# Adding up the kinds of edges in another stage of a graph and mixture-of-experts kernel

## The reference, cut to what matters

```python
edge_index = jnp.stack([src, dst])
xn = _layernorm(x, axis=-1)
x = x + _L0_gnn_ref(xn, edge_index, edge_type_8, ...) + _L0_mix_ref(xn[None], ...)[0]
x = x + _L0_ffn_ref(_layernorm(x, axis=-1)[None], ...)[0]
```

```python
self_idx = jnp.arange(num_nodes, dtype=edge_index.dtype)
ei = jnp.concatenate([edge_index, jnp.stack([self_idx, self_idx], axis=0)], axis=1)
row, col = (ei[0], ei[1])
deg = jnp.zeros((num_nodes,), dtype=h.dtype).at[row].add(1.0)
deg_inv_sqrt = deg ** (-0.5)
norm = deg_inv_sqrt[row] * deg_inv_sqrt[col]
```

## Time and profile before

| | before |
|---|---|
| median of 3 runs | 2826.07 us (2821.76 to 2828.15) |
| the profiled execution, its own time | 2828.88 us |
| its span | 2827.1 us |
| PE busy | 2438.5 us, 86% |
| PE weight loads (beside the products) | 1990.5 us, 70% |
| DVE busy | 1542.4 us, 55% |
| ACT busy | 910.1 us, 32% |
| GpSimd busy | 673.1 us, 24% |
| mean granted clock of PE | 0.93 of full |
| HBM traffic over the span | 148 GB/s |

### The profile page before, as it was taken

The page is one execution under the profiler, slowest core; times in us unless marked ns, Lnnn a source line. Parts: engine busy times, 40 slices in busy tenths (PEclk is TensorE's granted clock), DMA queues, the critical chain, the costliest instruction groups (busy, mean ns, idle before and its releaser), DMA issues.

```text
span 2827.1 us, 32184 instructions
## 1 busy us (share of the span) xinstructions
PE 2438.5 (86%) x12218; PEld 1990.5 (70%) x12218; DVE 1542.4 (55%) x2412; ACT 910.1 (32%) x1115; POOL 673.1 (24%) x408
## 2 busy tenths in 40 slices
PE   5898897889999999987888789886949999987775
PEld 4777796667777777766677678775737789775654
DVE  4897334323332333246799787655953234567674
ACT  2222232111111111121366666514723212225341
POOL 3355401200000000011244343204521100226451
PEclk9999999989999999999899899987979999998888
DMA  4144441522221221134787978557833322436561
GB/s 119 45 107 117 118 143 64 162 64 78 82 78 57 83 82 38 53 114 165 236 286 262 285 257 287 196 173 235 288 135 129 103 68 67 149 115 239 191 224 62
DMA packets 170651, 406.79 MB, mean 144 GB/s; under 512 B 70935, under 2 KB 71249, under 8 KB 170468
## 3 DMA queue, kind: packets, MB, share of 16 engines
q1 hardware_dynamic: 94598, 336.90, 35.6%
q0 software_dynamic: 20144, 41.82, 4.6%
q10 hardware_dynamic: 55726, 25.60, 3.4%
HBM read 360.49 MB, written 56.80 MB: 148 GB/s over the span
## 4 chain that ended last, share of the span: by engine, by line
PE 57%; DVE 19%; DMA 12%; issue 4%; ACT 3%; ACTq 2%; SPq 1%; DVEq 1%; POOL 1%; POOLq 0%
PE PS L290 12%; PE PS L291 12%; PE PS L292 11%; PE PS L1173 7%; DVE low L282 6%; PE PS L951 4%; DMA q_rows<-leaf_rows_k 2%; ACT high L269 2%; PE PS L546 1%; DVE expert_stats L332 1%; ACTq L479 1%; PE PS L1424 1%; PE PS L2226 1%; DMA x_base<-in_x 1%; PE PS L1789 1%
## 5 line engine op out<-in xcount | busy, mean ns | idle before, releaser
L269 ACT ACTIVATE high<-raw 128x1024 fp32r<-128x1024 f32 x532 | 542.7, 1055 | 431.2 <-PE PS L292 290.1
L282 DVE TENSOR_TENSOR low<-raw,high 128x1024 fp32r<-128x1024 f32 x388 | 574.5, 1506 | 165.2 <-ACT high L269 162.4
L290 PE MATMUL PS<-high,xt_high 128*125 128x512 f32 x1280 | 520.0, 406 | 57.7 <-DVE low L282 14.8
L291 PE MATMUL PS<-low,xt_high 128*125 128x512 f32 x1280 | 513.3, 401 | 0.0
L292 PE MATMUL PS<-high,xt_low 128*125 128x512 f32 x1280 | 511.4, 400 | 0.0
L282 POOL TENSOR_TENSOR low<-raw,high 128x1024 fp32r<-128x1024 f32 x144 | 373.4, 2593 | 488.7 <-ACT high L269 477.6
L290 PEld LDWEIGHTS PS<-high,xt_high 128*125 128x125 f32 x1280 | 242.5, 189 | 123.6 <-issue 19.8
L292 PEld LDWEIGHTS PS<-high,xt_low 128*125 128x125 f32 x1280 | 241.9, 189 | 62.9
L291 PEld LDWEIGHTS PS<-low,xt_high 128*125 128x125 f32 x1280 | 242.3, 189 | 57.9
L1206 DVE TENSOR_TENSOR y_low<-PS,y_high 125x512 fp32r<-125x512 f32 x80 | 55.3, 692 | 296.5 <-ACT y_high L1195 296.5
L1195 ACT ACTIVATE y_high<-PS 125x512 fp32r<-125x512 f32 x80 | 47.8, 598 | 525.0 <-PE PS L292 525.0
(11 more groups left out here) (508 smaller groups left out, 4298.9 us busy)
## 6 DMA issues: line engine op xcount, KB each, us to landing
raw<-in_L_ffn_ew SPq DMA_DIRECT2D x96, 512.0 KB, 5.8
raw<-in_L_gnn_weight SPq DMA_DIRECT2D x64, 512.0 KB, 5.8
raw<-in_L_ffn_k_w SPq DMA_DIRECT2D x64, 512.0 KB, 7.1
raw<-in_L_ffn_q_w SPq DMA_DIRECT2D x64, 512.0 KB, 10.9
raw<-in_L_ffn_v_w SPq DMA_DIRECT2D x64, 512.0 KB, 9.1
raw<-in_L_ffn_f_w SPq DMA_DIRECT2D x64, 512.0 KB, 7.3
adjacency<-a_stage ACTq DMA_DIRECT2D x10, 1250.0 KB
a_kind<-adjacency POOLq DMA_DIRECT2D x8, 1525.9 KB, 18.5
```

The costliest lines, as they stand in the source:

```text
L269: a.e.activation(HIGH[i % NHIGH][:, 0:w], RAW[PLACE_OF[i]][:, 0:w], ACT.Copy).then_inc(*a.step(part_high, 1, [("high", i)]))
L282: v.e.tensor_tensor(LOW[p][:, 0:w], RAW[p][:, 0:w], HIGH[i % NHIGH][:, 0:w], ALU.subtract).then_inc(*v.step(signal, 1, [("low", i)]))
L290: p.e.matmul(dst, xh[:, kt, xs], wh[:, c], start=first and j == 0, stop=False)
L291: p.e.matmul(dst, xh[:, kt, xs], wl[:, c], start=False, stop=False)
```

## The change

The sum over the kinds, its degrees and its transpose leave the counting stage. GpSimd adds nothing there and makes only the low parts 0 to 5 in the start; parts 6 to 27 become DVE's, which makes them at the end of each bucket's turn. DVE adds one kind at a time to a tile of 125 x 3125 in the relations, behind `y_low` of tile 10r + 9, from the `a_kind` tile that the aggregate reads. The degrees, and five blocks of 125 for the transpose, stand in the gates and are stored between the loads of SP. The tile of the sum takes room of four places, so the rings of places change from part 33 on, and with them the moments at which SP may load.

```diff
     RINGS = [(0, EARLY + [12, 13]),
-             (33, [7, 8, 9, 10, 11, 6, 12, 13, 0, 1, 2, 3, 4, 5]),
-             (107, [6, 0, 1, 2, 3, 4, 5, 7, 8, 9, 10]),
-             (131, LEAF_K + LEAF_Q + LAST + [1, 2, 3, 4, 5, 7, 8, 9, 10, 6, 0]),
-             (200, LEAF_Q + LAST + [1, 2, 3, 4, 5, 7, 8, 9, 10, 6, 0]),
-             (250, [1, 2, 3, 4, 5, 7, 8, 9, 10, 6, 0]),
-             (329, AFTER_K + LAST + [3, 4] + ROUTED + [5] + BASE),
-             (369, LAST + [3, 4, 5] + BASE)]
+             (33, [6, 0, 1, 2] + LAST + [3, 4, 5]),
+             (107, [3, 4, 5, 6, 0, 1, 2]),
+             (127, [7, 8, 9, 10]),
+             (131, LEAF_K + LEAF_Q + LAST + [2, 3, 4, 5, 6, 0, 1, 7, 8, 9, 10]),
+             (200, LEAF_Q + LAST + [2, 3, 4, 5, 6, 0, 1, 7, 8, 9, 10]),
+             (250, [2, 3, 4, 5, 6, 0, 1, 7, 8, 9, 10]),
+             (329, AFTER_K + LAST + [4, 5] + ROUTED + [6] + BASE),
+             (369, LAST + [4, 5, 6] + BASE)]
...
     def low_on_gpsimd(i):
-        return i < 28 or i in (123, 124, 125) or 126 < i < 388 and i % 4 == 3 or i > 438 and i % 2 == 1
+        return i < 6 or i in (123, 124, 125) or 126 < i < 388 and i % 4 == 3 or i > 438 and i % 2 == 1
...
-    def turn_sum_tensor(p, c):
-        ps = bank(6, 2).rearrange("p (m c) -> p m c", c=128)[0:64, 0:TT, 0:PT]
-        p.wait_ge(at("kinds", c), at("target", c - 1) if c else at("bounds"))
-        for m in range(TT):
-            ins = p.e.transpose(ps[:, m, :], ALLC[c % 3][:, m, :], ident[0:PT, 0:PT])
-        ins.then_inc(*p.mark("sum turned", c))
...
-            if b % 4 == 2 and b >= 10:
-                turn_sum_tensor(p, b // 4 - 2)
...
             if j == 0:
-                a.wait_ge(*[at("adj stored", c - 2), at("kinds", c - 2)] if c > 1 else [at("many"), at("bounds")])
+                a.wait_ge(*[at("adj stored", c - 2)] if c > 1 else [at("many"), at("bounds")])
...
+        low_parts(v, fill_to(1, 1))
...
+            low_parts(v, fill_to(3 + h, 1))
+        low_parts(v, fill_to(5, 1))
...
-    def turn_sum_vector(v, c):
-        e, ps = v.e, bank(6, 2).rearrange("p (m c) -> p m c", c=128)[0:64, 0:TT, 0:PT]
-        v.wait_ge(at("kinds", c), at("degree", c - 1) if c else at("degree one"))
-        e.tensor_reduce(deg[:, 1, :], ALLC[c % 3][:, :, :], axis=AX.X, op=ALU.add).then_inc(*v.mark("summed", c))
-        v.wait_ge(v.last)
-        e.tensor_tensor(deg[:, 0, :], deg[:, 0, :], deg[:, 1, :], ALU.add).then_inc(*v.mark("degree", c))
-        v.wait_ge(at("sum turned", c))
-        if c > 1:
-            v.wait_ge(at("adjt stored", c - 2))
-        e.scalar_tensor_tensor(TA[c % 2][:, :, :], iota16[0:64, 0:N].rearrange("p (m c) -> p m c", m=TT), tgt[:, c:c + 1], ps,
-                               op0=ALU.is_equal, op1=ALU.add).then_inc(*v.mark("target", c))
...
-            if b % 4 == 2 and b >= 10:
-                turn_sum_vector(v, b // 4 - 2)
             if b % 2 == 0 and b:
                 fill_out_vector(v, 5 + b // 2)
-        for n in range(25, 30):
-            fill_out_vector(v, n)
-        turn_sum_vector(v, 8)
-        turn_sum_vector(v, 9)
-        v.wait_ge(v.last)
-        rsqrt(v, deg[:, 0, :], dis[:, :], lnt[:, 6, :], lnt[:, 7, :], "degree root")
+            low_parts(v, fill_to(6 + b // 2, b % 2))
+        for n in range(26, 30):
+            low_parts(v, fill_to(n, 0))
+            fill_out_vector(v, n - 1)
+            low_parts(v, fill_to(n, 1))
+        fill_out_vector(v, 29)
...
-        g.wait_ge(g.last)
-        e.iota(tgti[:, :], [[64, 10]], base=0, channel_multiplier=1).then_inc(*g.mark("target iota"))
...
-        low_parts(g, fill_to(0, 1))
-        fill_out_gpsimd(g, 0)
-        low_parts(g, fill_to(1, 1))
-        fill_out_gpsimd(g, 1)
-        for h in range(2):
-            fill_out_gpsimd(g, 2 + h)
-            low_parts(g, fill_to(3 + h, 1))
-        low_parts(g, fill_to(5, 1))
+        low_parts(g, 6)
...
     def edges_gpsimd(g):
         e = g.e
-        fill_out_gpsimd(g, 4)
-        fill_out_gpsimd(g, 5)
-        for b in range(NB):
-            if b % 4 == 3:
-                c = b // 4
-                stg, total = STG[c % 2], ALLC[c % 3][:, :, :]
-                g.wait_ge(at("copied", b), at("many"), at("bounds"))
-                if c > 2:
-                    g.wait_ge(at("sum turned", c - 3), at("summed", c - 3))
-                g.wait_ge(g.last)
-                e.tensor_tensor(total, stg[:, :, 0, :], stg[:, :, 1, :], ALU.add).then_inc(*g.mark())
-                for r in range(2, 8):
-                    g.wait_ge(g.last)
-                    e.tensor_tensor(total, total, stg[:, :, r, :], ALU.add).then_inc(*g.mark(*("kinds", c) if r == 7 else ()))
-            if b % 2 == 0 and b:
-                fill_out_gpsimd(g, 5 + b // 2)
-            low_parts(g, fill_to(6 + b // 2, b % 2))
-        for n in range(26, 30):
-            low_parts(g, fill_to(n, 1))
+        for n in range(4, 10):
+            fill_out_gpsimd(g, n)
...
-    def turn_sum_sync(s, c):
-        s.wait_ge(at("target", c), s.before(tas[c % 2]))
-        s.e.dma_start(adjt[64 * c:64 * c + 64, :], TA[c % 2][:, :, :].rearrange("p m c -> p (m c)")).then_inc(*s.lands(tas[c % 2], "adjt stored", c))
...
             n = 6 + b // 2
-            if b % 4 == 2 and b >= 10:
-                turn_sum_sync(s, b // 4 - 2)
             if n % TT == TT - 1:
                 load_parts(s, 9 + 4 * (n // TT) + (2, 4)[b % 2])
         load_parts(s, 33)
-        turn_sum_sync(s, 8)
-        turn_sum_sync(s, 9)
...
     def counted():
 
-        return [at("adj stored", 8), at("adj stored", 9), at("counts stored", 18), at("counts stored", 19), at("adjt stored", 8),
-                at("adjt stored", 9), at("degree root"), at("root stored", 28), at("root stored", 29), at("k", 9)]
+        return [at("adj stored", 8), at("adj stored", 9), at("counts stored", 18), at("counts stored", 19), at("own column"), at("root stored", 28), at("root stored", 29), at("k", 9)]
...
     def mix0_sync(s):
         load_parts(s, 38, *counted())
-        load_parts(s, 46)
...
-                    load_parts(s, 50 + 4 * h)
+                    load_parts(s, 46 + 4 * h)
...
     GROUPS = [(r, h) for r in range(8) for h in range(2)]
+
+
+    ASUM = place("a_sum", [PT, TT, N], F32, SPARE)
+    TA = place("at_stage", [PT, TT, PT], F32, SPARE + 12512)
+    tgt = const("target_id", [PT, TT], F32)
...
+    def add_kind(v, r):
+        a = AR[r % 2][:, :, 0:N].bitcast(F32)
+        v.wait_ge(at("kind", r), v.last)
+        if r:
+            v.e.tensor_tensor(ASUM[:, :, :], ASUM[:, :, :], a, ALU.add).then_inc(*v.mark("kinds", r))
+        else:
+            v.e.tensor_copy(ASUM[:, :, :], a).then_inc(*v.mark("kinds", r))
+
+    def degrees_vector(v):
+        v.wait_ge(at("target iota"))
+        v.e.tensor_copy(tgt[:, :], tgti[:, :]).then_inc(*v.mark())
+        v.e.tensor_reduce(deg[:, :], ASUM[:, :, :], axis=AX.X, op=ALU.add).then_inc(*v.mark())
+        v.wait_ge(v.last)
+        v.e.tensor_scalar(deg[:, :], deg[:, :], 1.0, None, op0=ALU.add).then_inc(*v.mark())
+        v.wait_ge(v.last)
+        rsqrt(v, deg[:, :], dis[:, :], lnt[:, 6, :], lnt[:, 7, :], "degree root")
+
+    def turn_sum_tensor(p, j):
+        ps = bank(6, 2).rearrange("p (m c) -> p m c", c=128)[0:PT, 0:TT, 0:PT]
+        p.wait_ge(at("kinds", 7), at("target", j - 1) if j else at("xl", "u", 4))
+        for m in range(TT):
+            ins = p.e.transpose(ps[:, m, :], ASUM[:, m, cols(j)], ident[0:PT, 0:PT])
+        ins.then_inc(*p.mark("sum turned", j))
+
+    def turn_sum_vector(v, j):
+        ps = bank(6, 2).rearrange("p (m c) -> p m c", c=128)[0:PT, 0:TT, 0:PT]
+        v.wait_ge(at("sum turned", j), v.last)
+        if j:
+            v.wait_ge(at("adjt stored", j - 1))
+        v.e.scalar_tensor_tensor(TA[:, :, :], iota16[0:PT, 0:N].rearrange("p (m c) -> p m c", m=TT), tgt[:, j:j + 1], ps,
+                                 op0=ALU.is_equal, op1=ALU.add).then_inc(*v.mark("target", j))
+
+    def turn_sum_sync(s, j):
+        s.wait_ge(at("target", j), s.before(ta_sem))
+        s.e.dma_start(adjt[j * PT:(j + 1) * PT, :], TA[:, :, :].rearrange("p m c -> p (m c)")).then_inc(*s.lands(ta_sem, "adjt stored", j))
...
             make_y_vector(v, n)
+            if n % 10 == 9:
+                add_kind(v, n // 10)
...
     def load_kind(g, r):
         if r > 1:
-            g.wait_ge(at("agg", 10 * (r - 2) + 9))
+            g.wait_ge(at("agg", 10 * (r - 2) + 9), at("kinds", r - 2))
...
         for r in range(8):
             load_kind(g, r)
+        g.wait_ge(g.last)
+        g.e.iota(tgti[:, :], [[PT, TT]], base=0, channel_multiplier=1).then_inc(*g.mark("target iota"))
...
-        load_parts(s, 115)
+        load_parts(s, 114)
...
             gate_tensor(p, 0, t, 1)
             if t + 3 < TT:
                 delta_tensor(p, t + 3)
+            else:
+                turn_sum_tensor(p, t - 2)
         for t in range(TT):
             gate_tensor(p, 1, t, 0)
+            if t < 2:
```

(76 more changed lines are left out.)

6 lines of the change are left out of this document (1 added, 5 removed).

## The result

The changed kernel takes 2935.04 us (2931.08 to 2945.06, 4 runs) against 2825.97: ratio 1.0393, 95% interval 1.0364 to 1.0422, 109 us slower (111 by the ratio, which the experiments below are compared with). The prediction said 2874, with a range of 2842 to 2900. The direction was right, the size was not: less than half of the loss was foreseen. The profiled execution has a span of 2931.9 us, 104.8 longer than before, at a mean granted clock of 0.918.

What follows compares the result with a forecast made beforehand. TensorE (PE) was taken as the bound, busy throughout the relations and 94% in counting, with DVE at 90% there. Counting 12, mixer 5, relations 12, gates 7, nodes 12 made +48 on 2826.1: 2874 us, range 2842 to 2900.

Steps and rivals of the forecast that it cites:

- Counting, what is removed: Counting stage: GpSimd's adds and 50 transposes on PE go away, a gain of 8 us, bounds 3 and 27.
- rival A: Counting stage: the shared SBUF port is what costs, so the kernel gets faster, 2811 us; chance 0.05.
- Counting, what is added: Bucket loop: DVE's low parts wait for ACT ahead of the one-hots, DVE loses its lead; 20 us, bounds 10 and 26.
- First mixer: First mixer: parts 38 and 39 load only after four output tiles are stored; +5 us, bounds 2 and 9.
- Relations: Relations: DVE's adds of a kind delay low parts, PE stops 1.8 us at six boundaries; 12 us, bounds 8 and 13.
- Gates: Gates: degrees cost 0; waits around the transpose's stores 3, transposes on PE 3.5, part 119 1; +7 us, bounds 3 and 12.
- Nodes: Nodes: x1's first stores stand behind a load that waits for places used in gate(1,t,1); +12 us, bounds 7 and 20.
- The sum: Whole kernel: counting 12, mixer 5, relations 12, gates 7, nodes 12, together +48 us.
- +81: Whole kernel: all upper ends together, 23 + 9 + 13 + 16 + 20 us, called not likely.
- All four rivals: Whole kernel: A 2811 us (chance 0.05), B 2842 (0.12), C 2855 (0.2), D 2826 (0.03).

Runs made afterwards that it cites:

- low_gp: Changed kernel with low parts 6 to 27 back on GpSimd, in the order of the kernel before; adds stay away: 2893.33 us, ratio 1.0222.
- b_low_dve: Kernel before with only low parts 6 to 27 moved to DVE, at the change's places; adds stay on GpSimd: 2873.48 us, ratio 1.0155.
- mix40: Changed kernel with parts 38 and 39 loaded right behind part 37 in the first mixer, not behind four stores: 2928.38 us, ratio 1.0356.
- split_sum: Changed kernel with each kind added in five pieces of 625 columns behind tiles 10r+5 to 10r+9: 2924.84 us, ratio 1.0332.
- x_first: Changed kernel with SP's loads of parts 111 to 113 moved behind the first three x tiles: 2919.87 us, ratio 1.0327.
- turn_late: Changed kernel with the sum's five transpose blocks one behind each gate(1,t,0), their stores behind the loads of parts 114 to 118: 2922.74 us, ratio 1.0340.
- late127: Changed kernel without the load of parts 123 to 126 at the gates' end; they load behind x1's first two stores: 2925.92 us, ratio 1.0352.

## Why the prediction was wrong in size

**Counting, what is removed.** The term was 8 us; measured are 11.6 (low_gp) and 10.4 (b_low_dve against the changed kernel), inside the bounds of 3 and 27. The Trainium skill (GPSIMD Engine Reference, Specifications) has GpSimd and VectorE share SBUF interfaces; the one-hot's mean of 248 against 458 ns agrees. By that alone (rival A) the stage would have become faster. It holds for the instruction, but the order in the queue decided the kernel's time.

**Counting, what is added.** One of the two steps that failed: mis-sized by 25 us. Its mechanism was right, down to the bucket: counted from bucket 15, bucket 18 was to end 25.2 us later, and ended 25.9 later (202.60 to 228.54). Its sum of 20 measured 45. From the ends of the buckets, the four groups with low parts lost (change of the difference to before): buckets 6 to 10 7.0 where I had 2.6, 16 to 20 8.6 (7), 26 to 31 11.7 (4), 36 to 39 10.2 (7), together 37.5. These are net of what the missing work on the sum wins there. Against low_gp, where it is missing too, they lost 13.0, 9.4, 16.3 and 11.5, less 4.2 in bucket 35 and 1.3 elsewhere: the 45. I had taken 26 to 31 as a repetition of 16 to 20 at a lower price, though it has two holds of ACT's queue, 5.70 and 5.42 us in the trace after. And I had the colder clock only in the upper bound of 26: the granted clock of 200 to 300 us was 0.97 before and is 0.90 in the windows above.

**First mixer.** 8 against 5, within its bounds of 2 and 9; the stop of 9.45 us in front of part 38 is the foreseen one, and mix40 takes it away.

**Relations.** Addition 3.42 us as worked out (3.4), stop 2.02 instead of 1.8, and seven of them: the copy of kind 0 cost as much as an add, which I had only as an upper end. That makes 14.1 where the term had 12. Most of the other 6 us is clock: from stop to stop it takes 81.4 us three times and 82.9 to 83.0 three times, 4.7 us in all, though PE waited the same 2.02 us. The windows of the changed kernel around a stop of the second kind (736.50) and of the first (819.46) show it in the granted clock:

```profile
700.00:750.00 50.00, 47.98 (x200) 37.84 (x200) 16.86 (x18) 7.49 (x10) 0.00 (x0) 0.97 0.13 43
...
800.00:850.00 50.00, 47.98 (x208) 38.00 (x207) 16.04 (x16) 8.00 (x11) 1.65 (x1) 1.00 0.19 63
```

Just behind the two stops it is the lower of the clock's two levels, half of full, against full:

```profile
736.70:739.90 3.20, 3.20 (x8) 2.45 (x8) 0.79 (x1) 0.58 (x2) 0.00 (x0) 0.50 0.03 5
819.60:822.80 3.20, 3.20 (x15) 2.56 (x16) 1.65 (x3) 1.55 (x2) 0.00 (x0) 1.00 0.03 5
```

The same 3.2 us touch 8 matrix products at the one and 15 at the other. The term had no room for that; 20 lies above its upper end of 13. The Trainium skill (VectorE: DVE Perf Modes, The perf-mode tier table) gives fp32 copies twice the rate of adds. The copy of 5 x 625 elements took 3.41 us beside 3.42 for the add, while the pieces of 625 in split_sum took 486 ns beside 810. So the copy of 5 x 625 was not at that rate, and the small ones were close to it. The large one read 5 rows with a gap between them and wrote one run of 3125; which of these matters was not tried. The 1.3 us that I gave for this can't be redone from the rows: a stop of 1.8 behind 3.4 us leaves 1.6 of slack, so a copy at twice the rate would have cost some 0.2 in place of 1.8.

**Gates.** The step that failed in kind, and the one furthest off: 35 us against 7. I wrote that the new order issues the x tile before the gate weights, "so it lands about 6 us sooner". That was read from `gates_sync` alone. `relations_sync` ends with `load_parts(114)`, and with 7 places the parts 111 to 113 take those of 104 to 106, which are used until `gate(0,4,0)`; everything of `gates_sync` stands behind them. The x tiles came later, not sooner. For 115 and 116, in the same ring, I did follow the tenants. x_first gives 19 us back. The rest of the term was right in its mechanism (the store of block 0 behind 115, DVE waiting for it, PE for DVE), but is worth 12.7 us in turn_late where I had a net of 3: I had two stops of 3 and 4 us less 4 of old ones (2.67 and 1.34 in the trace before), and the trace after has three, of 3.29, 5.80 and 5.03 us.

**Nodes.** 15 against 12, by the mechanism that was foreseen; late127 wins 10.3 of it in the trace and 12 in the time.

**The sum.** 33 + 8 + 20 + 35 + 15 = 111, against 48. The second layer gave back 7. That is no effect of the change that I can name: from the last transpose of `u_rows` to the end, the kernel before takes 1480 us, and the changed kernel and its variants, with the same code there, take 1473 (the changed kernel) to 1490 (split_sum). All five terms came out above their forecasts, and their sum above the +81 that the prediction had called unlikely since the terms are independent. All four rivals lay on the other side.

## What to carry to other kernels

An instruction that waits for another engine costs its queue the lead it had, whatever its own length: 16 low parts of 1.2 us, inside the loop over the buckets, cost 45 us ahead of the one-hots and nothing two buckets later. When a ring of places is made smaller, list for each load the tenant that it waits for and then everything behind it in that queue, across the stage's border too. And a stop of PE can have a second price in its clock: here three of seven stops of 2 us cost 1.6 us more, so that the row was worth more than its sum.
